# Masked keys of a small self-attention as four diagonal blocks, and a new slot order for its steps

## The chip, the cores and the metric

The kernel runs on one core of one Trainium2 chip. The engines of the core are TensorE (PE in the profile, with PEld for its weight loads), VectorE (DVE), ScalarE (ACT), GpSimd (POOL) and SyncE (SP, which issues the DMAs here). The metric is the device time of the program in microseconds, the median of several runs; lower is better.

## The reference

The program computes six residual steps on x (64 sequences of 32 tokens, width 256): cross-attention, windowed self-attention, a quantised FFN, a second cross-attention, a causal self-attention with a geometric bias, and a four-matrix FFN. The fifth is the one that the change touches:

```
qkv = (x @ Wqkv + bqkv)                       # x: layer-normed, 64 x 32 x 256; 16 heads of 16
std_logits   = einsum('bhid,bhjd->bhij', q, k) * dh ** (-0.5)
p1, p2       = x @ W1p, x @ W2p               # 4 numbers per head
lines_h      = plucker_lines(p1, p2)          # 6 products per head, divided by their norm
plucker_bias = einsum('bhic,bhjc->bhij', lines_h, lines_h @ _J6.T)
logits       = std_logits + plucker_bias * plucker_scale
attn = softmax(where(causal, -inf, logits));  out = (attn @ v) @ Wout + bout
```

## The kernel before, in words

Tokens lie in 16 tiles of 128 rows, four sequences of 32 tokens each. The fifth step, called A1 in the code, handles the tiles one after the other in four **lanes** (tile n is lane n mod 4); each lane has its own buffers and its own pair of PSUM banks, `bank[l][0]` and `bank[l][1]`. For each tile, in this order:

- ScalarE normalises x (`a_scale`), TensorE turns the tile (`p_turn`), ScalarE copies it (`a_xnT`), and TensorE multiplies by all weights (`p_project`; L548 and L554).
- VectorE puts q and k with their bias into slots of 32 columns per head (`d_slots`). ScalarE copies p1 and p2 out (`a_lines`), GpSimd forms the six products (`lines`, L2083 to L2089), VectorE sums their squares (`d_lines`), and GpSimd takes the norm's inverse and writes the line numbers into the slots (`lines_unit`, L2093 to L2102). GpSimd also adds the output bias (`bias`, L1948).
- TensorE turns the slots of q and k into the two banks (`p_slots`, L598 and L603). Now each 32-row group of `bank[l][1]` holds the keys of one head in a group of four heads. ScalarE copies the queries (`a_keys`, L1085). VectorE writes the **masked keys** (`d_keys`, L1407): a tile `kbd` of 128 x 2048 that repeats the keys four times and multiplies them by a 0/1 mask, so that only the diagonal 32-row blocks are not zero.
- TensorE multiplies (`p_scores`, L617). VectorE masks, takes the maximum and subtracts it (`d_mask` L1451, `d_max` L1456, `d_shift` L1460), ScalarE takes the exponential (`a_exp`, L1124), VectorE the sums (`d_sums`).
- TensorE turns the probabilities (`p_turn_probs`, L638), ScalarE copies them (`a_pT`, L1128), TensorE multiplies by the values (`p_values`, L648), VectorE normalises (`d_norm_out`, L1474), TensorE turns (`p_turn_out`, L657), ScalarE copies (`a_oT`), TensorE multiplies by Wout (`p_out`, L554), and VectorE adds to x (`d_add`, L1488). The values themselves are copied by ScalarE (`a_values`), turned by VectorE (`d_turn_values`) and spread by ScalarE (`a_spread_values`, L1074).

Each engine runs its own list in order and waits on semaphores. The order is set by a table of **slots**: a round has 28 slots, each lane starts 7 slots after the one before, and each engine has a list of (slot, step). So with T for the tile whose scores are next, each engine repeats one fixed sequence of steps of neighbouring tiles per 7 slots. Slots of two engines are not tied to each other except by the semaphores. `between` tables put single steps of the last FFN's start into the last round: the row statistics of the first block (`two_stats`, `g_aggregate`, `g_rsqrt`, `g_normalise`) and its first matmuls (`g_turn`, `g_pair`).

```
SLOTS0, SLOTS1 = 20, 28
lag = slots // NL
kbd = [view(a[2], 2048) for a in lane_at]
om = [view(a[2], D) for a in lane_at]
```

`om`, the normalised output of `d_norm_out`, lies over the first 256 columns of `kbd`.

Of the kernel before, what the change touches and what calls it, by code (L numbers as in the profile page):

```python
# [15 lines left out]
P = 128  # L16
# [27 lines left out]
def perceiver(nc, A, out):  # L44
    ctx = ExitStack()
    with ctx:
# [75 lines left out]
        om = [view(a[2], D) for a in lane_at]  # L122
        kT = [view(a[3], D) for a in lane_at]
# [278 lines left out]

        def halves(ap):
            return ap.rearrange("p (a b) -> p a b", b=P)
# [134 lines left out]
        def _(pe):  # L539
# [23 lines left out]
            def p_project(kind, l, n):  # L563
# [3 lines left out]
                if kind == A1:  # L567
                    project_rows(bank[l][0], xnT[l], a1_wqkv[:, :, 0:2 * D]).then_inc(s["qk_ready"], 1)
                    project_rows(bank[l][1][:, D:D + 8 * H], xnT[l],
                                 a1_wpl[:, :, :, :].rearrange("p k a b -> p k (a b)"))  # L570
                    for fo in range(KI):
                        r = project(vb[:, fo, :], a1_wqkv[:, :, 2 * D:3 * D], xnT[l], fo)
                    r.then_inc(s["v_ready"], 1)
                    return
# [78 lines left out]
            def p_turn_out(kind, l, n):  # L653

                pe.wait_ge(s["o_normed"], tile(n, l))
                for half in range(KI):
                    r = tr(bank[l][0][:, D + half * P:D + (half + 1) * P], om[l][:, half * P:(half + 1) * P], ident[:])  # L657
                r.then_inc(s["oT_ready"], 1)
# [351 lines left out]
            def g_last(b):  # L1010
                for t in range(TPB):
                    pe.wait_ge(g_c, quadrant_no(8 * b + 7, 12 if t >= 2 else 21))
                    at = slice(t % 2 * P, t % 2 * P + P)
                    for k in range(NF1):
# [7 lines left out]
                                (4, lambda l, i: p_project_last(A1, l, i + BASE[A1]))]  # L1022
                 + attention(A1, "a1", [(12, p_slots), (15, p_scores), (20, p_turn_probs),
                                        (22, p_values), (24, p_turn_out), (26, p_out)])[1])],
# [22 lines left out]
        def _(act):  # L1047
# [34 lines left out]
            def a_keys(kind, l, n):  # L1082
                if kind == A1:
                    act.wait_ge(s["qk_slots_ready"], tile(n - BASE[A1], l))
                    af(qT1[l], bank[l][0], ACT.Copy).then_inc(s["qT_copied"], 1)  # L1085
                    return
# [263 lines left out]
            def g_close(b, h, f):  # L1350
# [13 lines left out]
                (1, a_scale), (5, a_xnT), (9, a_lines), (12, a_values), (16, a_spread_values),  # L1364
                (18, a_keys), (23, a_exp), (24, a_pT), (27, a_oT))])], {("tail", 6): lambda: g_turned(0)})
# [17 lines left out]
        def _(dve):  # L1383
# [17 lines left out]
            def d_keys(kind, l, i, n):  # L1401

                if kind == A1:
                    dve.wait_ge(s["qk_slots_ready"], tile(n - BASE[A1], l))
                    k = bank[l][1].rearrange("p (c k) -> p c k", k=L).unsqueeze(2).broadcast_to([P, H, J, L])
                    m = mask4[:, :].unsqueeze(1).unsqueeze(3).broadcast_to([P, H, J, L])
                    v.tensor_tensor(kbd[l].rearrange("p (c j k) -> p c j k", j=J, k=L), k, m, ALU.mult)\  # L1407
                        .then_inc(s["k_masked"], 1)
# [61 lines left out]
            def d_norm_out(kind, l, i, n):  # L1470
# [3 lines left out]
                v.tensor_tensor(om[l].rearrange("p (h e) -> p h e", e=HD),  # L1474
# [323 lines left out]
            dve.wait_ge(consts_made, 6)  # L1798
# [4 lines left out]
            d_turn_values(A1, 0, 0, BASE[A1])  # L1803
            c_add(T - 1)
# [97 lines left out]
            def g_last(b):  # L1902
# [7 lines left out]
                (3, d_slots), (8, d_lines), (8, d_turn_values), (13, d_keys), (16, d_mask),  # L1910
                (16, d_max), (17, d_shift), (18, d_sums), (22, d_norm_out), (26, d_add))])],
# [16 lines left out]
        def _(pool):  # L1928
# [131 lines left out]
            for i in range(1, T - 1):  # L2060
                for u in range(SPT):
                    c_step(i, u, False, False)
                    n = SPT * i + u
                    for m, n0 in enumerate((8, 28)):
                        if n0 <= n < n0 + 8:
                            quadrant_sum(m, n - n0)
            for u, l in enumerate((0, 1, 3, 2)):
# [5 lines left out]
            pool.wait_ge(consts_made, 6)  # L2073
# [42 lines left out]
            def g_rsqrt(b):  # L2116
# [7 lines left out]
                (14, of_last(lines)), (17, lambda l, i: b_bias(A1, l, i)), (18, of_last(lines_unit))])],  # L2124
                      {("last", 18): lambda: g_rsqrt(0)})
# [90 lines left out]
```

## Time and profile before

| | us |
|---|---|
| median of 3 runs | 1551.03 (1550.93 to 1554.02) |
| the profiled execution, its own time | 1552.65 |
| its span, first to last instruction | 1550.8 |
| PE busy in the span | 1454.3 (94%) |
| DVE busy | 893.5 (58%) |
| ACT busy | 711.6 (46%) |
| POOL busy | 504.1 (33%) |

A1 stands between about 830 and 997 us of the span. Shares over the whole span say little about it: it is a sixth of the time and has its own limits, so it is read by its own chain of waits and timeline. "The granted clock" is the share of full speed that TensorE had in a stretch.

### The profile page before, as it was taken

What the parts mean: (1) busy time and instruction counts of PE and PEld (TensorE: products, weight loads), DVE (VectorE), ACT (ScalarE), POOL (GpSimd) and SP (SyncE); (2) the same over time, 40 slices, a digit from 0 to 9 for tenths busy, and PEclk for the clock granted to TensorE, in tenths of its full rate; (3) what the DMA queues carried; (4) which work ended last, traced back from release to release, by engine and by line L of the source; (5) the groups of instructions that cost most, each with busy time, mean ns of one, the idle gap of its engine ahead of it and who ended that gap; (6) DMA issues with size and microseconds to landing.
All of it is one profiled execution on the core that took longest, in us unless ns stands there. A gap on an engine that the chain in (4) does not pass through costs nothing.

```text
span 1550.8 us, 32878 instructions
## 1 busy us (share of the span) xinstructions
PE 1454.3 (94%) x12566; PEld 1126.0 (73%) x12566; DVE 893.5 (58%) x1892; ACT 711.6 (46%) x1767; POOL 504.1 (33%) x698
## 2 busy tenths in 40 slices
PE   6999998998999999999997888899999999999998
PEld 5877776456777777777775666578858876885887
DVE  5988997499446666666665887543234224323332
ACT  6887777498545555555553655322211211221221
POOL 2445552001037956965656777100000000000000
PEclk9999999999999999999998999999999999999999
DMA  8000000007031262146110000124404421441240
GB/s 304 21 7 2 1 1 21 0 7 220 18 145 54 69 249 60 42 169 230 48 41 1 2 0 2 49 87 139 155 14 142 143 109 48 143 143 62 95 143 14
DMA packets 60521, 124.13 MB, mean 80 GB/s; under 512 B 5009, under 2 KB 15761, under 8 KB 57873
## 3 DMA queue, kind: packets, MB, share of 16 engines
q1 hardware_dynamic: 60432, 122.94, 23.0%
q8 instruction: 57, 0.93, 0.3%
q14 instruction: 32, 0.25, 0.1%
HBM read 108.24 MB, written 14.68 MB: 79 GB/s over the span
## 4 chain that ended last, share of the span: by engine, by line
PE 69%; DVE 14%; POOL 8%; issue 5%; ACT 3%; DVEq 0%; DMA 0%; SPq 0%; POOLq 0%; ACTq 0%
PE ps L965 24%; PE ps L548 15%; PE ps L768 5%; PE ps L554 5%; PE ps L762 4%; PE ps L1016 4%; PE ps L788 3%; POOL R L2051 2%; PE ps L740 2%; POOL R L2033 2%; DVE R L1727 2%; DVE R L1407 2%; PE ps L799 2%; DVE amax L1594 1%; POOL R L2025 1%
## 5 line engine op out<-in xcount | busy, mean ns | idle before, releaser
L965 PE MATMUL ps<-R 128*128 128x256 f32 x1792 | 388.6, 379 | 3.4 <-DVE R L1875 3.4
L965 PEld LDWEIGHTS ps<-R 128*128 128x128 f32 x1792 | 340.0, 190 | 52.3 <-issue 6.5
L548 PE MATMUL ps<-R 128*128 128x128 f32 (+1 forms) x1344 | 306.3, 387 | 1.8 <-ACT R L1080 0.9
L548 PEld LDWEIGHTS ps<-R 128*128 128x128 f32 x1344 | 189.7, 194 | 110.2 <-issue 105.2
L1283 ACT ACTIVATE R<-ps,c_nmx 128x257 f32<-128x257 f32 x256 | 118.2, 474 | 126.4 <-DVE c_nmx L1751 126.4
L2033 POOL TENSOR_TENSOR R<-R,c_inv 128x1024 f32<-128x1024 f32 x64 | 121.1, 1892 | 130.9 <-DVE c_inv L1762 130.9
L1727 DVE COPY R<-ps 128x512 f32<-128x512 f32 x128 | 88.2, 689 | 82.3 <-PE ps L788 81.0
L768 PE MATMUL ps<-x_wv,R 128*128 128x256 f32 x512 | 121.1, 379 | 0.0
L2119 POOL TENSOR_SCALAR g_ve<-g_mv 128x4 f32<-128x4 f32 x4 | 1.0, 238 | 336.2 <-DVE g_mv L1824 336.2
L768 PEld LDWEIGHTS ps<-x_wv,R 128*128 128x128 f32 x512 | 92.5, 190 | 10.1
L762 PE MATMUL ps<-R,x_wk 128*128 128x256 f32 x384 | 95.6, 391 | 0.0
L1355 ACT ACTIVATE R<-R,ffn_s 128x256 f32<-128x256 f32 x32 | 16.3, 509 | 167.8 <-DVE R L1882 167.8
L788 PE MATMUL ps<-ident,R 128*128 128x128 f32 x512 | 80.1, 280 | 7.9 <-POOL R L2033 3.8
L1751 DVE TENSOR_REDUCE c_nmx<-ps 128x2 f32<-128x514 f32 x128 | 82.5, 686 | 1.6 <-PE ps L778 1.5
L762 PEld LDWEIGHTS ps<-R,x_wk 128*128 128x128 f32 x384 | 68.9, 189 | 12.2 <-issue 0.4
L788 PEld LDWEIGHTS ps<-ident,R 128*128 128x128 f32 x512 | 61.0, 142 | 21.7 <-issue 7.8
L1342 ACT ACTIVATE R<-ps,ffn_s 128x512 f32<-128x512 f32 x32 | 21.9, 687 | 114.9 <-PE ps L548 114.5
L1275 ACT ACTIVATE R<-ps 128x512 f32<-128x512 f32 x64 | 38.4, 600 | 75.3 <-PE ps L768 75.3
L1594 DVE TENSOR_REDUCE amax<-R 128x1 f32<-128x512 f32 (+1 forms) x60 | 58.3, 1002 | 23.7 <-ACT R L1170 23.2
L2025 POOL TENSOR_TENSOR R<-R 128x512 f32<-128x512 f32 x64 | 67.3, 1053 | 9.0 <-DMA R<-in_ctxT 9.0
L799 PEld LDWEIGHTS ps<-R 128*32 128x32 f32 x2048 | 32.4, 110 | 43.4 <-DVE R L1727 31.7
L1860 DVE SCALAR_TENSOR_TENSOR R<-ps,ffn_s,R 128x512 f32<-128x512 f32 x32 | 24.0, 750 | 59.4 <-ACT R L1342 59.4
(219 smaller groups left out, 2515.1 us busy)
## 6 DMA issues: line engine op xcount, KB each, us to landing
R<-quadrant_sums SPq DMA_DIRECT2D x32, 1024.0 KB, 6.8
R<-in_f_hq SPq DMA_DIRECT2D x32, 768.0 KB, 4.5
R<-in_ctxT SPq DMA_DIRECT2D x64, 257.0 KB, 2.7
R<-in_f_hq SPq DMA_DIRECT2D x8, 1024.0 KB, 8.7
quadrant_sums<-R SPq DMA_DIRECT2D x8, 1024.0 KB, 8.2
R<-in_ctxT SPq DMA_DIRECT2D x16, 256.0 KB, 3.9
k_ahead<-R SPq DMA_DIRECT2D x16, 256.0 KB, 3.8
R<-k_ahead SPq DMA_DIRECT2D x16, 256.0 KB, 3.1
```

What stands on the lines that cost most here:

```text
L548: r = mm(dst, w[:, ki, fo * P:(fo + 1) * P], src[:, ki, :], start=(ki == 0), stop=(ki == KI - 1))
L554: r = mm(dst, src[:, ki, :], w[:, ki], start=(ki == 0), stop=(ki == KI - 1))
L762: r = mm(ps[:, 4, fo * D:(fo + 1) * D], x1_wk[:, ki, fo * P:(fo + 1) * P], c_ctx[u][:, ki, 0:2 * P], start=(ki == 0), stop=(ki == KI - 1))
L768: r = mm(ps[:, 5, c * D:(c + 1) * D], c_ctx[u][:, ki, c * P:(c + 1) * P], x1_wv[:, ki, :], start=(ki == 0), stop=(ki == KI - 1))
L788: r = tr(ps[:, 6, at:at + P], c_p[par][:, g, c * P:(c + 1) * P], ident[:])
L965: r = mm(ps[:, 4 * (g % 2) + bk, half * HALF:(half + 1) * HALF], f_wr[g % 3][:, w, ki * P:(ki + 1) * P], src[:, k, ki, :], start=(ki == 0) ...
L1283: af(c_p[par][:, g, :], ps[:, g, 0:S], ACT.Exp, bias=c_nmx[par][:, g:g + 1], accum_out=c_sum[par][:, g:g + 1]).then_inc(c_exp, 1)
L1594: v.tensor_reduce(o, i, AX.X, ALU.max, apply_absolute_value=True).then_inc(f0_ugm, 1)
L1727: v.tensor_copy(c_pT[:, 2 * k:2 * k + 2, :, :].rearrange("p g c t -> p (g c t)"), ps[:, 6, :])\
L1751: v.tensor_reduce(c_nmx[u % 2][:, 2 * half:2 * half + 2], ps[:, 2 * half:2 * half + 2, 0:S], AX.X, ALU.max, negate=True).then_inc(c_max, 1)
L2025: p.tensor_tensor(c_ctx[u][:, :, 0:S - 1], c_ctx[u][:, :, 0:S - 1], c_ctx[u][:, :, S - 1:S].broadcast_to([P, KI, S - 1]), ALU.subtract).th ...
L2033: p.tensor_tensor(c_p[u % 2][:, :, 0:S - 1], c_p[u % 2][:, :, 0:S - 1], c_inv[u % 2][:, :].unsqueeze(2).broadcast_to([P, G, S - 1]), ALU.m ...
```

## The change

Instead of one multiplication by the mask, the masked keys become four copies of a diagonal block of 32 rows x 16 heads x 32 columns, from PSUM into `kbd`. VectorE copies blocks 0 and 1, ScalarE blocks 2 and 3 (behind its copy of the queries). The rest of `kbd` is zero: it is written once per lane by a memset of 128 x 2048, two on GpSimd inside the second cross-attention (after its sequences 48 and 52), one on GpSimd behind the last slot memset, one on VectorE in front of `c_add` of the last tile. So that nothing overwrites the zeros, A1's normalised output moves to `om1`, over the scores' buffer. `p_project` gets a wait for the x update of the lane's tile before. All four engines get other slots.

```
+        om1 = [view(a[5], D) for a in lane_at]
...
+        def key_block(l, j):
+            return kbd[l][j * L:(j + 1) * L, :].rearrange("p (c j k) -> p c j k", j=J, k=L)[:, :, j, :]
+        def key_rows(l, j):
+            return bank[l][1][j * L:(j + 1) * L, :].rearrange("p (c k) -> p c k", k=L)
...
                 if kind == A1:
+                    pe.wait_ge(s["x_updated"], tile(n - 1, l))
                     project_rows(bank[l][0], xnT[l], a1_wqkv[:, :, 0:2 * D]).then_inc(s["qk_ready"], 1)
...
-                                (4, lambda l, i: p_project_last(A1, l, i + BASE[A1]))]
-                 + attention(A1, "a1", [(12, p_slots), (15, p_scores), (20, p_turn_probs),
-                                        (22, p_values), (24, p_turn_out), (26, p_out)])[1])],
+                                (2, lambda l, i: p_project_last(A1, l, i + BASE[A1]))]
+                 + attention(A1, "a1", [(11, p_slots), (15, p_scores), (18, p_turn_probs),
+                                        (21, p_values), (23, p_turn_out), (26, p_out)])[1])],
...
                     act.wait_ge(s["qk_slots_ready"], tile(n - BASE[A1], l))
-                    af(qT1[l], bank[l][0], ACT.Copy).then_inc(s["qT_copied"], 1)
+                    af(qT1[l], bank[l][0], ACT.Copy)
+                    for j in (2, 3):
+                        r = af(key_block(l, j), key_rows(l, j), ACT.Copy)
+                    r.then_inc(s["qT_copied"], 1)
...
-                    v.tensor_tensor(kbd[l].rearrange("p (c j k) -> p c j k", j=J, k=L), k, m, ALU.mult)\
-                        .then_inc(s["k_masked"], 1)
+                    for j in (0, 1):
+                        r = v.tensor_copy(key_block(l, j), key_rows(l, j))
+                    r.then_inc(s["k_masked"], 1)
...
+            v.memset(kbd[3], 0.0).then_inc(consts_made, 1)
             c_add(T - 1)
...
-                (3, d_slots), (8, d_lines), (8, d_turn_values), (13, d_keys), (16, d_mask),
-                (16, d_max), (17, d_shift), (18, d_sums), (22, d_norm_out), (26, d_add))])],
+                (2, d_slots), (5, d_lines), (8, d_turn_values), (11, d_keys), (15, d_mask),
+                (15, d_max), (15, d_shift), (18, d_sums), (19, d_norm_out), (27, d_add))])],
...
+                    if n in (48, 52):
+                        p.memset(kbd[(n - 48) // 4], 0.0).then_inc(consts_made, 1)
...
-                (14, of_last(lines)), (17, lambda l, i: b_bias(A1, l, i)), (18, of_last(lines_unit))])],
-                      {("last", 18): lambda: g_rsqrt(0)})
+                (4, of_last(lines)), (12, lambda l, i: b_bias(A1, l, i)), (9, of_last(lines_unit))])],
+                      {("last", 16): lambda: g_rsqrt(0)})
```

ScalarE's table changes in the same way. What the tables do to the lists is seen in the program's rows. On TensorE, one repetition in the middle of A1 before: the probabilities' turn (L638) stands behind the output product (L554 with `a_wout`) and the slots (L598, L603).

```order
L617 MATMUL ps<-R 32x2x2x32 [waits qT_copied,k_masked]
L657 MATMUL ps<-ident,R 128x128 [waits o_normed]
L554 MATMUL ps<-a_wqkv,R 128x512 [waits xnT_copied]
L554 MATMUL ps<-a_wpl,R 128x128 x2
L548 MATMUL ps<-R,a_wqkv 128x128 x4
L554 MATMUL ps<-a_wout,R 128x256 [waits oT_copied]
L598 MATMUL ps<-ident,R 128x128 [waits q_slots]
L603 MATMUL ps<-ident,R 128x128 [waits v_copied]
L638 MATMUL ps<-ident,R 128x128 [waits probs_ready]
L560 MATMUL ps<-ident,R 128x128 [waits xn_ready]
L648 MATMUL ps<-R 32x4x16 [waits pT_copied,v_spread]
```

And the same repetition now (lines are 8 to 10 higher; L626 is the scores, L562 the products, L647 the probabilities' turn, L607 and L612 the slots, L657 the values, L568 the first turn):

```order
L626 MATMUL ps<-R 32x2x2x32 [waits qT_copied,k_masked]
L666 MATMUL ps<-ident,R 128x128 [waits o_normed]
L562 MATMUL ps<-a_wqkv,R 128x512 [waits x_updated,xnT_copied]
L562 MATMUL ps<-a_wpl,R 128x128 x2
L556 MATMUL ps<-R,a_wqkv 128x128 x4
L647 MATMUL ps<-ident,R 128x128 [waits probs_ready]
L607 MATMUL ps<-ident,R 128x128 [waits q_slots]
L612 MATMUL ps<-ident,R 128x128 [waits v_copied]
L562 MATMUL ps<-a_wout,R 128x256 [waits oT_copied]
L657 MATMUL ps<-R 32x4x16 [waits pT_copied,v_spread]
L568 MATMUL ps<-ident,R 128x128 [waits xn_ready]
```

The probabilities' turn moved ahead of the slots, and the output product behind them. On GpSimd in the last round, before, the FFN's row statistics (L2119, L2121) stand in front of a tile's `lines` (L2083):

```order
L2097 TENSOR_TENSOR R<-R,lrn 128x96 [waits q_evac,lines_step]
L2101 COPY R<-R 128x16x6 [waits lines_step]
L2102 TENSOR_TENSOR R<-R,plsc 128x16x6
L2119 TENSOR_SCALAR g_ve<-g_mv 128x4 [waits mv_ready]
L2121 TENSOR_TENSOR g_rstd<-g_ve,minus_half 128x4 [waits vare_ready]
L2083 TENSOR_TENSOR R<-R 128x16x3 [waits lines_in]
```

Now the same pair (L2139, L2141) stands one tile later, between `lines_unit` of tile 13 and `lines` of tile 14:

```order
L2117 TENSOR_TENSOR R<-R,lrn 128x96 [waits q_evac,lines_step]
L2121 COPY R<-R 128x16x6 [waits lines_step]
L2122 TENSOR_TENSOR R<-R,plsc 128x16x6
L2139 TENSOR_SCALAR g_ve<-g_mv 128x4 [waits mv_ready]
L2141 TENSOR_TENSOR g_rstd<-g_ve,minus_half 128x4 [waits vare_ready]
L2103 TENSOR_TENSOR R<-R 128x16x3 [waits lines_in]
```

Before, the pair was between tiles 12 and 13; the DVE statistics that it waits for stood behind `d_keys` of tile 12 and now stand in front of `d_mask` of tile 12.

## Rows read from the trace of the kernel before

**Rows 1.** Busy time by engine in one stretch: us, PE, PEld, DVE, ACT, POOL, PEclk, DMA

```profile
900.00:910.00 10.00, 8.52 (x132) 6.70 (x132) 8.70 (x18) 5.46 (x15) 7.41 (x15) 1.00 0.00 0
```

**Rows 2.** Chain of waits, one repetition of A1: start us, us, what

```profile
909.03 1.08 PE ps L617 x32
910.11 0.37 PE ps L657 x2
910.48 2.16 PE ps L554 x8
912.64 0.89 PE ps L548 x8
913.54 0.86 PE ps L554 x4
914.40 0.44 PE ps L598 x4
914.84 0.45 PE ps L603 x4
915.31 2.30 DVE R L1407
...
949.79 0.45 PE ps L638 x4
```

**Rows 3.** Timeline in the middle of A1: start us, us, engine, line, op, [idle before <-releaser]

```profile
897.48 1.42 POOL L2083 TENSOR_TENSOR R<-R 128x48 f32<-128x48 f32 x6 [0.96 <-ACT R L1111]
...
901.05 2.91 POOL L2093 TENSOR_TENSOR lrn<-lsq,minus_half 128x16 f32<-128x16 f32 x1 [0.57 <-DVE lsq L1436]
...
901.55 0.69 DVE L1451 SCALAR_TENSOR_TENSOR R<-ps,causal 128x512 f32<-128x512 f32 x1 [0.21 <-PE ps L617]
...
903.72 0.63 ACT L1124 ACTIVATE R<-R 128x512 f32<-128x512 f32 x1 [0.93 <-DVE R L1460]
...
904.78 0.37 POOL L2102 TENSOR_TENSOR R<-R,plsc 128x96 f32<-128x96 f32 x1
...
907.12 0.60 ACT L1128 ACTIVATE R<-ps 128x512 f32<-128x512 f32 x1 [1.01 <-PE ps L638]
907.62 0.60 ACT L1085 ACTIVATE R<-ps 128x512 f32<-128x512 f32 x1
...
907.86 0.65 PE L648 MATMUL ps<-R 128*32 128x64 f32 x32 [0.56 <-ACT R L1128]
```

**Rows 4.** Groups of instructions by line: busy us, mean ns of one | idle before

```profile
L1727 DVE COPY R<-ps 128x512 f32<-128x512 f32 x128 | 88.2, 689 | 82.3 <-PE ps L788 81.0
L2072 POOL MEMSET R<- 128x1024 f32 x4 | 3.8, 952 | 0.0
L1074 ACT ACTIVATE R<-R,mask 128x256 f32<-128x256 f32 x64 | 27.1, 494 | 2.3 <-DVE R L1419 2.3
```

**Rows 5.** Timeline: around two of the places where memsets go

```profile
744.20 1.89 POOL L2033 TENSOR_TENSOR R<-R,c_inv 128x1024 f32<-128x1024 f32 x1 [0.26 <-DVE c_inv L1762]
...
748.48 0.60 PE L788 MATMUL ps<-ident,R 128*128 128x128 f32 x4
...
843.03 0.42 DVE L1745 TENSOR_TENSOR x<-x,ps 128x256 f32<-128x256 f32 x1 [2.51 <-PE ps L554]
```

**Rows 6.** Timeline: scores of tiles 1, 12 and 13 on PE

```profile
857.10 1.08 PE L617 MATMUL ps<-R 128*32 128x128 f32 x32 [0.51 <-DVE R L1407]
...
952.18 1.08 PE L617 MATMUL ps<-R 128*32 128x128 f32 x32 [0.52 <-DVE R L1407]
...
965.24 1.08 PE L617 MATMUL ps<-R 128*32 128x128 f32 x32
```

**Rows 7.** Timeline: the row statistics on GpSimd, and TensorE after them

```profile
952.61 0.25 POOL L2119 TENSOR_SCALAR g_ve<-g_mv 128x4 f32<-128x4 f32 x1 [4.23 <-DVE g_mv L1824]
952.94 1.04 POOL L2121 TENSOR_TENSOR g_rstd<-g_ve,minus_half 128x4 f32<-128x4 f32 x1
...
960.89 1.11 PE L598 MATMUL ps<-ident,R 128*128 128x128 f32 x4 [3.34 <-POOL R L2101]
```

More of the change, by code:

```diff
@@ L656, in p_turn_out @@
                 for half in range(KI):
-                    r = tr(bank[l][0][:, D + half * P:D + (half + 1) * P], om[l][:, half * P:(half + 1) * P], ident[:])
+                    r = tr(bank[l][0][:, D + half * P:D + (half + 1) * P], (om1 if kind == A1 else om)[l][:, half * P:(half + 1) * P],
+                           ident[:])
                 r.then_inc(s["oT_ready"], 1)
@@ L1084, in a_keys @@
                     act.wait_ge(s["qk_slots_ready"], tile(n - BASE[A1], l))
-                    af(qT1[l], bank[l][0], ACT.Copy).then_inc(s["qT_copied"], 1)
+                    if isinstance(n, int) and n == BASE[A1]:
+                        act.wait_ge(consts_made, 10)
+                    af(qT1[l], bank[l][0], ACT.Copy)
+                    for j in (2, 3):
+                        r = af(key_block(l, j), key_rows(l, j), ACT.Copy)
+                    r.then_inc(s["qT_copied"], 1)
                     return
@@ L1363, in _ @@
             run_lanes(act, SLOTS1, [(lambda: None, [(at, of_last(step)) for at, step in (
[L1364 to L1365 removed]
+                (0, a_scale), (3, a_xnT), (9, a_lines), (11, a_values), (18, a_spread_values),
+                (17, a_keys), (20, a_exp), (24, a_pT), (27, a_oT))])], {("tail", 6): lambda: g_turned(0)})
             for l in range(NL):
@@ L1404, in d_keys @@
                     dve.wait_ge(s["qk_slots_ready"], tile(n - BASE[A1], l))
-                    k = bank[l][1].rearrange("p (c k) -> p c k", k=L).unsqueeze(2).broadcast_to([P, H, J, L])
-                    m = mask4[:, :].unsqueeze(1).unsqueeze(3).broadcast_to([P, H, J, L])
-                    v.tensor_tensor(kbd[l].rearrange("p (c j k) -> p c j k", j=J, k=L), k, m, ALU.mult)\
-                        .then_inc(s["k_masked"], 1)
+                    if isinstance(n, int) and n == BASE[A1]:
+                        dve.wait_ge(consts_made, 10)
+                    for j in (0, 1):
+                        r = v.tensor_copy(key_block(l, j), key_rows(l, j))
+                    r.then_inc(s["k_masked"], 1)
                     return
@@ L1473, in d_norm_out @@
                 dve.wait_ge(s["o_ready"], tile(n, l))
-                v.tensor_tensor(om[l].rearrange("p (h e) -> p h e", e=HD),
+                v.tensor_tensor((om1 if kind == A1 else om)[l].rearrange("p (h e) -> p h e", e=HD),
                                 bank[l][0][:, 0:D].rearrange("p (h e) -> p h e", e=HD),
@@ L1797, in _ @@
             c_evacuate(NSEQ - 1, 0)
-            dve.wait_ge(consts_made, 6)
+            dve.wait_ge(consts_made, 8)
             d_slots(A1, 0, 0, BASE[A1])
@@ L2072, in _ @@
                 p.memset(slots_of[l], 0.0).then_inc(consts_made, 1)
-            pool.wait_ge(consts_made, 6)
+            p.memset(kbd[2], 0.0).then_inc(consts_made, 1)
+            pool.wait_ge(consts_made, 8)
             pool.wait_ge(later_made, 3)
```

## The prediction, made before the changed kernel was run

> **What bounds the kernel now.** I read the self-attention stage A1 alone, in four steps. First the busy time by engine in one stretch of ten microseconds [rows 1]: TensorE 8.52, VectorE 8.70, GpSimd 7.41, ScalarE 5.46. No engine is full, so the stage is bound by a loop of waits that passes over engines, and the chain of waits has to show it. It does [rows 2]: from the start of one tile's scores (L617) to the next tile's it reads scores 1.08, turn of the output 0.37, projections 2.16 + 0.89, output product 0.86, the two turns of the slots 0.44 + 0.45, the masked keys on VectorE 2.30, and then scores again. That is 8.55 us and 0.08 between the pieces, 8.63 a tile. The scores of tiles 1 and 12 start at 857.10 and 952.18 [rows 6]: 95.08 over 11 tiles, 8.64. So the loop holds for the whole middle, and of its parts only the keys are not TensorE's. While they are made, TensorE does what it has (turns, values) and idles for the rest; part of it is a wait of 0.56 for the copied probabilities [rows 3].
>
> Second, the end of the stage. Between the scores of tiles 12 and 13 lie 13.06 us [rows 6], 4.42 more than a period. GpSimd stood 4.23 us in front of the row statistics of the next FFN, which wait for VectorE behind the keys of tile 12; so it began the lines of tile 13 late, and TensorE stood 3.34 us for the slots of tile 13. After that its four turns took 1.11 us, where the chain gives 0.44 in the middle [rows 2, 7]: a wait of this length is also paid in clock.
>
> **The keys.** The one instruction of 2.30 us on the loop goes. VectorE gets two copies of 32 x 512 from PSUM, ScalarE two of the same size behind its copy of the queries. No row shows 32 partitions at work. The nearest for VectorE is its copy of 128 x 512 from PSUM, 0.689 [rows 4]; two are 1.38. For ScalarE two copies of 128 x 512 from PSUM stand back to back, each of 0.60 and 0.50 apart [rows 3]; three in a row take 0.50 + 0.50 + 0.60 = 1.60. Both start when the slots are turned, so ScalarE ends last and 1.60 takes the place of 2.30. From below: were fewer partitions cheaper, the queries' copy alone still takes 0.60, and TensorE's own work between the slots and the scores would decide (below). From above: the spread of the values writes short runs, 0.494 for 256 elements [rows 4], so 0.99 for 512; then ScalarE takes 0.50 + 2 x 0.99 = 2.5. I take 1.60, since engine, source and size are those of its rows and only the partitions differ.
>
> The trace has 2.30 for 2048 elements in one instruction and 0.689 for 512, so four pieces cost 2.76 of engine time. The Trainium skill warns of this on the page "VectorE: DVE Perf Modes" (section "The TRN2 errata — SBUF-src ops pay a fixed extra latency per instruction"): the fixed cost is paid by each instruction, so many small tiles are dear. Were all four pieces on VectorE, the keys' step would be 2.76 and the loop longer than now; by the rows it shrinks only because two engines work side by side.
>
> **The loop after the new slots.** TensorE's list now has the turn of the probabilities (0.45) where the output product (0.86) was; the product stands behind the slots, beside the keys. The loop is 1.08 + 0.37 + 2.16 + 0.89 + 0.45 + 0.44 + 0.45 = 5.84, plus 1.60 for the keys and 0.08: **7.52 us**. Beside the keys TensorE has the product 0.86, the values 0.65 at most and one turn of about 0.2, in sum 1.7: as long as the keys. So its own work is about as long as the loop, and nothing much below 7.4 can come of it. What else has to be ready in time:
> - Probabilities. From the mask (901.55) to the exponential's end (903.72 + 0.63) it is 2.80 [rows 3]; with 0.07 ahead and 0.05 behind, 2.92 after the scores. The cover was turn, projections, product and slots; now it is the turn and the projections, 0.37 + 3.05 = 3.42. Hidden, with 0.5 to spare; behind this wait stand the slots, the product, the values and the next scores.
> - VectorE: 8.70 in ten is 7.5 a tile; less 2.30, plus 1.38 makes 6.6 of 7.52. ScalarE: 4.7 plus 1.2 makes 5.9. ScalarE's exponential now stands behind spread, values and the output's copy of its list; these end about 2.8 us after the scores' start, the shift ends at 3.3.
> - GpSimd: lines and bias from 897.48 to 900.48 (901.05 less the idle 0.57), 3.00, and the unit from 901.05 to 905.15, 4.10 [rows 3]: 7.1 of 7.52. It fits, but with only 0.4 a tile.
> - The new wait for the x update in front of the projections: that addition ends some five microseconds before, it costs nothing. Behind it stands all of TensorE's list.
> Gain: 8.64 - 7.52 = 1.12 a tile.
>
> **The memsets.** A memset of 1024 on GpSimd takes 0.952 [rows 4]; 2048 lie between that and 1.90. The first, behind sequence 48, would push the normalisation at 744.20 by at most 1.64; it would end at 747.7, and TensorE turns its result at 748.48 [rows 5]: hidden, with 0.75 left. The same pattern repeats behind sequence 52. The third stands where GpSimd waits for A1's first lines. If that cover were gone, each would cost up to 1.9. VectorE's memset is not in the trace; a 2048-element instruction takes 2.30 there [rows 2], and it falls into an idle stretch of 2.51 in front of L1745 [rows 5]. I count all four as nothing.
>
> **The sum.** From the scores of tile 1 to those of 14 are 13 periods: 13 x 1.12 = 14.6. The excess of 4.4 at tile 13 goes, since GpSimd meets the statistics one tile later, when VectorE has long made them. Put back: two pairs of statistics and the aggregation on VectorE, which has less room now, about 0.6; and GpSimd's 0.25 + 1.04 with gaps = 1.4 [rows 7], against 0.4 of room a tile, about 0.8 at tile 14. The last two tiles, whose steps alternate with matmuls of the FFN, gain 0.7 each on their keys, and TensorE waits about 0.4 more for the last probabilities, whose turn now stands ahead of a product: +1.0. The first tile's keys: +0.7. In sum 14.6 + 4.4 - 1.4 + 1.0 + 0.7 = **19.3 us**. The profiled execution's span goes from 1550.8 to 1531.5 and its time from 1552.65 to 1533.4. The median was 1.6 below the latter, 1551.03, so the forecast is **1531.7**. A measurement of this kernel can tell about 0.2%, 3.1 us, from no change.
>
> **Rivals.**
> 1. The small room is used up, and another engine's loop ends last. GpSimd has 0.4 a tile, the probabilities 0.5. VectorE's sums of squares wait for GpSimd's lines, and the next tile's mask stands behind them; if they come 0.9 us late, TensorE waits at the probabilities each time. For it: GpSimd was idle 0.96 + 0.57 a tile, and 1.1 of that goes with the period. Against: the sum of its work is below 7.52. With a period of 7.9 and 1.9 put back at the end: 13 x 0.74 + 4.4 - 1.9 + 1.0 + 0.7 = 13.8, so 1537.2.
> 2. ScalarE's blocks cost 1 us each, by their written pattern (0.494 for 256), or because both engines now read one PSUM bank at a time, which they don't do before, and ScalarE waits 1.38 for VectorE: keys of 2.5, period 8.4. 13 x 0.24 + 4.4 - 0.5 + 0.7 = 7.7, so 1543.3. 
> 3. Better: the end puts nothing back and the period is TensorE's own 7.4: 13 x 1.24 + 4.4 + 1.0 + 0.7 = 22.2, so 1528.8.
> 4. Slower than before: a block of 32 rows costs ScalarE 1.5 us, three times what its size says. Then the keys take 3.5, the period is 5.84 + 3.5 + 0.08 = 9.4, and 13 x 0.78 = 10.1 is lost against 4.4 won: 1556.7. A tile gets longer from a block of 1.1 us (5.84 + 0.50 + 2.2 + 0.08 = 8.6), and the whole from 1.3, where 13 x 0.4 outweighs the stall's end. Against: the dearest row of ScalarE per element [rows 4] gives 0.99.
>
> **How the numbers follow.** Forecast 0.50, first rival 0.23, second 0.10, third 0.09, fourth 0.03; 0.05 for an end within 0.2%, where a period near 8.4 meets memsets that are not hidden. The forecast with the first and third rival makes 0.82, and reaches, with 1.5 us for their own spread, from 1527.5 to 1540; the second's bound is partly in it up to a period of 8.1, so I take 1527 to 1541. Faster by over 0.2%: 0.91, within: 0.05, slower: 0.04.
>
> **What would show it.** In the profile after: ScalarE's block copies at 0.60 and VectorE's at 0.69; the scores of tiles 2 to 12 at 7.5 apart; in the chain the keys' step on ScalarE's line, or no keys at all where TensorE's work fills it; no wait of GpSimd at the statistics and none of 3 us at the slots of tile 13; the second cross-attention as long as before. A period with a wait of the probabilities' turn (L647) or of the slots (L607) in it means the first rival, block copies of 1 us the second. The forecast is wrong if the gain isn't in A1's middle.

## The result

| | before, us | after, us |
|---|---|---|
| median | 1552.25 (4 runs) | 1537.4 (4 runs, 1535.16 to 1539.34) |
| profiled execution, own time | 1552.65 | 1535.16 |
| its span | 1550.8 | 1533.4 |

The ratio is 0.9906, with a 95% interval of 0.9893 to 0.992: 14.6 us less (0.94%). Between the two profiled executions it is 17.5. The prediction was 1531.7 with a range of 1527 to 1541 and a gain of 19.3. Direction and range held; the median is 5.7 above the forecast time, and the gain is 4.7 less than forecast.

The busy time of the same stretch as in [rows 1], in the changed kernel (columns as there: PE, PEld, DVE, ACT, POOL, clock):

```profile
900.00:910.00 10.00, 9.68 (x164) 7.23 (x166) 8.40 (x20) 8.68 (x21) 8.34 (x18) 1.00 0.00 0
```

TensorE went from 8.52 to 9.68 of ten: it is nearly the bound now. ScalarE went from 5.46 to 8.68. The chain of waits, one repetition, answers [rows 2] (L626 scores, L666 turn of the output, L562 and L556 projections, L647 turn of the probabilities, L607 and L612 slots, L1097 queries and L1099 two key blocks on ScalarE):

```profile
917.08 1.08 PE ps L626 x32
918.16 0.37 PE ps L666 x2
918.53 2.16 PE ps L562 x8
920.70 0.89 PE ps L556 x8
921.59 0.44 PE ps L647 x4
922.03 0.44 PE ps L607 x4
922.46 0.45 PE ps L612 x4
922.94 0.60 ACT R L1097
923.55 0.59 ACT R L1099
924.15 0.60 ACT R L1099
924.75 0.14 issue
924.88 1.08 PE ps L626 x32
```

This is the loop of the prediction, piece by piece, with two differences: the keys take 1.80 and not 1.60, and 0.14 follows them. 7.80 us in sum. The timeline of the same place shows what else stood near the end of the loop: VectorE's two blocks took their 1.38 and were done at 924.32, TensorE's own list was done at 924.72, ScalarE at 924.74.

```profile
922.94 0.60 ACT L1097 ACTIVATE R<-ps 128x512 f32<-128x512 f32 x1 [0.28 <-PE ps L612]
922.94 1.38 DVE L1423 COPY R<-ps 32x512 f32<-32x512 f32 x2 [0.70 <-PE ps L612]
923.55 1.19 ACT L1099 ACTIVATE R<-ps 32x512 f32<-32x512 f32 x2
923.70 0.65 PE L657 MATMUL ps<-R 128*32 128x64 f32 x32
924.28 0.44 PE L568 MATMUL ps<-ident,R 128*128 128x128 f32 x2
924.88 1.08 PE L626 MATMUL ps<-R 128*32 128x128 f32 x32 [0.16 <-ACT R L1099]
```

I took the start of the scores of every tile from the timelines and give the steps between them, for all kernels that follow too (one execution of each). "End" is from the scores of tile 15 to the start of the last output product, "sum" from the scores of tile 1 to there (before: 857.10 to 995.71; after: 854.89 to 978.28).

| kernel | mean of 1 to 11 | 11-12 | 12-13 | 13-14 | 14-15 | end | sum |
|---|---|---|---|---|---|---|---|
| before | 8.64 | 8.63 | 13.06 | 8.62 | 11.23 | 10.62 | 138.61 |
| after | 7.78 | 8.10 | 8.10 | 8.62 | 9.29 | 11.49 | 123.39 |
| after, second set of runs | 7.78 | 8.09 | 8.10 | 8.62 | 9.30 | 11.49 | 123.40 |
| blocks in the old order | 9.28 | 9.15 | 11.38 | 9.15 | 9.18 | 10.64 | 142.35 |
| the same, turn first | 8.64 | 8.66 | 11.92 | 8.74 | 9.19 | 10.64 | 135.57 |
| new order, one product | 8.25 | 8.76 | 8.75 | 8.64 | 10.92 | 11.49 | 131.07 |
| before, g_rsqrt later | 8.64 | 8.63 | 8.63 | 8.63 | 9.51 | 10.63 | 132.48 |
| two blocks left out | 7.59 | 7.57 | 7.56 | 8.15 | 9.90 | 11.49 | 120.59 |
| ScalarE's blocks from the queries' bank | 7.78 | 8.09 | 8.09 | 8.65 | 10.97 | 11.48 | 125.10 |
| ScalarE's blocks 128 rows | 7.59 | 8.10 | 8.10 | 8.62 | 9.52 | 11.49 | 121.76 |
| ScalarE's blocks, same rows | 7.66 | 8.10 | 8.10 | 8.63 | 9.42 | 11.48 | 122.32 |
| four blocks on VectorE | 9.00 | 11.20 | 9.51 | 8.72 | 9.67 | 11.49 | 140.60 |
| statistics before the keys | 7.78 | 7.79 | 7.80 | 8.28 | 9.29 | 11.49 | 122.44 |
| statistics earlier still | 7.78 | 7.80 | 8.60 | 7.80 | 9.29 | 11.49 | 122.79 |

So A1 from the scores of tile 1 on is 15.2 us shorter in this pair of profiles. The step from tile 0 to tile 1 went from 9.47 to 9.11. The other 1.8 us between the two profiled spans lie ahead of A1's scores, in a stretch whose steps on TensorE are the same in both kernels. Busy time and clock of that stretch, before and after:

```profile
800.00:830.00 30.00, 24.94 (x338) 18.37 (x337) 18.45 (x44) 14.62 (x50) 16.26 (x16) 0.90 0.04 10
```

```profile
800.00:830.00 30.00, 24.16 (x340) 18.13 (x339) 18.52 (x45) 14.60 (x50) 16.73 (x16) 0.97 0.04 10
```

The granted clock was 0.90 in the one and 0.97 in the other. In the second set of runs of the changed kernel the first scores started at 847.45, where the profile above has 845.78 and before 847.63, and A1 was the same to 0.01 us. That part is no gain of the change.

The step 14-15 holds a second difference of this kind. In the kernel before and in the same kernel with only `g_rsqrt` later, TensorE waits as long for the slots of this step (2.05 and 2.04), and then the same four matmuls take:

```profile
981.22 3.47 PE L548 MATMUL ps<-R 128*128 128x512 f32 x4
```

```profile
977.81 1.88 PE L548 MATMUL ps<-R 128*128 128x512 f32 x4
```

The granted clock was 0.68 in the first (979.70 to 985.09) and 1.00 in the second (976.40 to 980.09). The changed kernel and the one whose ScalarE reads the queries' bank differ in the same way without any stall before: 9.29 at a clock of 1.00 (961.50 to 966.79), 10.97 at 0.75 (963.70 to 970.66), behind equal waits of 1.61. So of the 1.94 that the step 14-15 fell from before to after, about 1.6 is clock (3.47 less 1.88), and no run shows it to belong to the change. Both clock differences widen the gap between the two profiled executions (17.5) beyond that of all runs (14.6).

### The profile page after: what moved, and what is told of

It reads as the page before. It is cut to its first block, busy times and chain, and to the rows that moved or that the text cites. A ratio compares the mean times of both kernels' runs of the same rounds, so it can differ in the third digit from the quotient of the medians.

```text
span 1533.4 us, 32957 instructions
## 1 busy us (share of the span) xinstructions
PE 1450.5 (95%) x12566; PEld 1122.4 (73%) x12566; DVE 880.5 (57%) x1909; ACT 732.6 (48%) x1799; POOL 507.2 (33%) x701
## 4 chain that ended last, share of the span: by engine, by line
PE 69%; DVE 12%; POOL 9%; issue 5%; ACT 3%; DVEq 0%; DMA 0%; SPq 0%; POOLq 0%; ACTq 0%
PE ps L975 24%; PE ps L556 15%; PE ps L778 5%; PE ps L562 4%; PE ps L772 4%; PE ps L1026 4%; PE ps L798 3%; POOL R L2068 2%; PE ps L750 2%; DVE R L1743 2%; POOL R L2050 2%; PE ps L809 2%; DVE amax L1610 1%; POOL R L2042 1%; PE ps L657 1%
## 5 line engine op out<-in xcount | busy, mean ns | idle before, releaser
L556 PE MATMUL ps<-R 128*128 128x128 f32 (+1 forms) x1344 | 305.2, 386 | 1.8 <-ACT R L1090 0.9
L556 PEld LDWEIGHTS ps<-R 128*128 128x128 f32 x1344 | 189.7, 194 | 109.8 <-issue 104.6
L2139 POOL TENSOR_SCALAR g_ve<-g_mv 128x4 f32<-128x4 f32 x4 | 0.9, 236 | 331.1 <-DVE g_mv L1841 331.1
```

The lines of the kernel that those rows point to most:

```text
L556: r = mm(dst, w[:, ki, fo * P:(fo + 1) * P], src[:, ki, :], start=(ki == 0), stop=(ki == KI - 1))
```

## The end of the stage

In the last tiles the chain leaves the loop of TensorE and ScalarE and goes over GpSimd (L2103 to L2109 the lines, L1965 the bias, L2113 to L2122 the unit):

```profile
929.78 1.42 POOL R L2103 x6
...
932.08 0.68 POOL x L1965
932.76 1.00 issue
933.80 2.92 POOL lrn L2113
936.79 0.36 POOL R L2117
...
937.90 1.41 POOL R L2103 x6
```

From one tile's lines to the next tile's it is 8.12 us. The "issue" of 1.00 is a wait for VectorE's sums of squares, which stand behind the FFN's row statistics. The timeline names it, beside the statistics that cause it:

```profile
932.15 0.75 DVE L1835 BATCH_NORM_STATS2 g_stats<-x 128x6 f32<-128x256 f32 x2
932.93 0.42 DVE L1490 TENSOR_TENSOR R<-ps,rinv 128x256 f32<-128x256 f32 x1
933.80 2.91 POOL L2113 TENSOR_TENSOR lrn<-lsq,minus_half 128x16 f32<-128x16 f32 x1 [1.04 <-DVE lsq L1452]
```

In the middle this wait is 0.39. GpSimd's own two instructions, which stood behind a wait of 4.23 in [rows 7], now stand behind none; but the x update behind the lines comes late, and TensorE waits for it:

```profile
946.09 0.25 POOL L2139 TENSOR_SCALAR g_ve<-g_mv 128x4 f32<-128x4 f32 x1
946.42 1.04 POOL L2141 TENSOR_TENSOR g_rstd<-g_ve,minus_half 128x4 f32<-128x4 f32 x1
...
949.76 0.25 DVE L1450 TENSOR_REDUCE lsq<-R 128x16 f32<-128x96 f32 x1 [0.85 <-POOL R L2109]
...
950.36 0.41 DVE L1504 TENSOR_TENSOR x<-x,ps 128x256 f32<-128x256 f32 x1
...
950.92 1.95 PE L562 MATMUL ps<-a_wqkv,R 128*128 128x512 f32 x4 [0.59 <-DVE x L1504]
```

## Experiments: which part of the change gives the gain

**Blocks alone.** The changed kernel with all slots of the kernel before.

```
-(11, p_slots), (15, p_scores), (18, p_turn_probs), (21, p_values), (23, p_turn_out), (26, p_out)
+(12, p_slots), (15, p_scores), (20, p_turn_probs), (22, p_values), (24, p_turn_out), (26, p_out)
...
-(18, a_spread_values), (17, a_keys), (20, a_exp), (24, a_pT), (27, a_oT)
+(16, a_spread_values), (18, a_keys), (23, a_exp), (24, a_pT), (27, a_oT)
```

> The changed kernel with the four blocks, om1 and the memsets, but with all slots of the kernel before (g_rsqrt at slot 18 too). Theory 1, each part is worth what its own place in the loop says: the keys' step shrinks from 2.30 to the 1.80 that ScalarE's three copies take in the trace of after (0.60 each, end to end), the rest of the loop stays, so the period is 8.13 and not 8.64; 13 x 0.5 = 6.5 us and about 1 more at the first and last tiles; the stall in front of the scores of tile 13 (13.06 for one tile before) stays near 12.6, and GpSimd stands over 4 us at the row statistics. About 1545, 7 us below before. Theory 2, the blocks pay only together with the order (another wait of the old list, such as the probabilities, fills the 0.5): period near 8.6, time within 1.5 us of before.

Measured: 1559.73 against 1552.15, ratio 1.0056 (1.0035 to 1.0076). The blocks alone make the kernel slower by 7.6 us, and both theories missed: a tile takes 9.15 and not 8.13. The timeline shows why (L647 turn of the probabilities, L1143 their copy):

```profile
903.16 0.60 PE L612 MATMUL ps<-ident,R 128*128 128x128 f32 x4
...
903.59 0.60 PE L647 MATMUL ps<-ident,R 128*128 128x128 f32 x4
903.80 1.38 DVE L1423 COPY R<-ps 32x512 f32<-32x512 f32 x2 [0.22 <-PE ps L612]
...
904.23 0.60 ACT L1143 ACTIVATE R<-ps 128x512 f32<-128x512 f32 x1 [1.02 <-PE ps L647]
904.73 0.59 ACT L1097 ACTIVATE R<-ps 128x512 f32<-128x512 f32 x1
```

VectorE starts its blocks at 903.80. ScalarE's list has the copy of the probabilities ahead of the keys, and this copy waits for TensorE's turn, which stands behind the slots. So ScalarE idles 1.02 and begins the queries at 904.73, 0.93 behind VectorE; from there its 1.80 decide. Before, ScalarE's queries were a single short copy beside 2.30 on VectorE, and this queue cost nothing. The blocks put ScalarE on the loop, and with it whatever is queued ahead of them.

**One place of TensorE's list.** The old order again, with the turn of the probabilities ahead of the slots.

```
-(12, p_slots), (15, p_scores), (20, p_turn_probs)
+(12, p_slots), (15, p_scores), (19, p_turn_probs)
```

> The four blocks in the order of before, with one place of TensorE's list changed: the turn of the probabilities stands ahead of the slots' turns (slot 19 and not 20), behind the output product. Theory 1: in the old order ScalarE's keys were queued behind its copy of the probabilities, which waited for TensorE's turn behind the slots; with the turn ahead of the slots that copy is done when the slots are, the queries' copy starts 0.06 to 0.3 behind them, and the period falls from 9.15 to 5.84 + 0.86 + 1.80 + 0.14 = 8.64; about 1553 to 1554, as much as before. Theory 2, ScalarE's list is not what costs: the probabilities are not ready ahead of the slots (2.92 after the scores), TensorE waits there, and the period stays at 9.1.

Measured: 1550.09 against 1551.03, ratio 0.9994 (0.998 to 1.0009), period 8.64 to the hundredth. Theory 1 holds for the period and for "as much as before"; its 1553 to 1554 was 3 to 4 too high (the steps 12-13 and 14-15 are 11.92 and 9.19, where before has 13.06 and 11.23). ScalarE's queue was the cost, and this one place of the new order pays for it. The rest of the way from 8.64 to 7.78 is as long as the output product (0.86), which the new order moves beside the keys; no run moves this product alone.

**Order alone.** The changed kernel with the masked keys as one product on VectorE.

```
-for j in (0, 1):
-    r = v.tensor_copy(key_block(l, j), key_rows(l, j))
...
+v.tensor_tensor(kbd[l].rearrange("p (c j k) -> p c j k", j=J, k=L), k, m, ALU.mult)
...
-for j in (2, 3):
-    r = af(key_block(l, j), key_rows(l, j), ACT.Copy)
```

> The changed kernel with its new slots and om1, but the masked keys as one multiplication of 128 x 2048 on VectorE, as before; ScalarE copies only the queries. Theory 1: the loop is after's with 2.30 in the place of 1.80, so 7.79 + 0.50 = 8.29 a tile; 0.35 a tile is won on before over 11 tiles (3.8), and the stall of 4.4 at tile 13 is gone because GpSimd meets the statistics a tile later; less 1 to 2 us in the last tiles. About 1545.5, 6 to 7 us below before, and with the gain of the blocks in the old order the sum is near the 14.6 of the whole change. Theory 2: the order brings only the stall (the turn of the probabilities, 0.45, takes the place of the output product, but VectorE is too full): period 8.6, about 1548.

Measured: 1546.49 against 1552.15, ratio 0.9964 (0.9955 to 0.9974), 5.7 us less; periods of 8.25. Theory 1 holds. The two parts don't add up, they need each other: in the old order the blocks change the period from 8.64 to 9.15, in the new one from 8.25 to 7.78.

**The stall at tile 13.** The kernel before with one number changed.

```
-{("last", 18): lambda: g_rsqrt(0)}
+{("last", 25): lambda: g_rsqrt(0)}
```

> The kernel before with one number changed: GpSimd's g_rsqrt stands at slot 25 of the last round and not at 18, so one tile later. Theory 1: the excess of 4.4 us in front of the scores of tile 13 is this wait alone; it goes, GpSimd's two instructions cost about 1.3 us against 1.5 of room a tile (8.64 less 7.1), so 0 to 0.5 comes back a tile later: about 1548, 4 to 4.4 below before. Theory 2: the excess belongs to something else in the last round (the VectorE statistics, the clock): it stays or moves to tile 14, and the time is within 1 us of before.

Measured: 1547.6 against 1552.15, ratio 0.9978 (0.9968 to 0.9988), 4.6 us less. Theory 1 holds: 13.06 became 8.63, and nothing came back at tile 14. The step 14-15 also fell, from 11.23 to 9.51, but that is the granted clock shown under the table. So this number alone is worth 4.4 us in the trace, beside 4.6 in the medians, and that is about three tenths of the 15.2 by which A1 got shorter.

## Experiments: why a tile takes 7.78 and not 7.52

The queries' copy and the two blocks stand 0.60 apart. In [rows 3] two full copies stand 0.50 apart. What takes the overlap away?

**Another bank.** ScalarE's blocks read the queries' bank.

```
-r = af(key_block(l, j), key_rows(l, j), ACT.Copy)
+r = af(key_block(l, j), bank[l][0][j * L:(j + 1) * L, :].rearrange("p (c k) -> p c k", k=L), ACT.Copy)
```

> The changed kernel, but ScalarE's two block copies read rows 64 to 127 of the queries' bank and not of the keys' bank, so that VectorE and ScalarE no longer read one bank together; the values of two blocks are not the keys (that part of the result is changed), sizes and places written stay. Theory 1, the missing overlap (0.60 apart and not 0.50, so 1.80 for the three copies and not 1.60) comes with copies of 32 rows and not with the shared bank: still 1.80. Theory 2, the shared bank holds ScalarE up: 1.60, and 0.50 between the starts of copies.

```profile
901.71 0.60 ACT L1097 ACTIVATE R<-ps 128x512 f32<-128x512 f32 x1 [0.28 <-PE ps L612]
902.32 1.19 ACT L1099 ACTIVATE R<-ps 32x512 f32<-32x512 f32 x2
```

Still 1.80 and 7.78 a tile (one run, 1539.05; its longer step 14-15 is the clock of 0.75 told above). The shared bank costs nothing. The Trainium skill ("PSUM — Partial Sum Buffer", section "PSUM bank collisions raise a hardware error") has accesses to different groups of 32 rows of one bank as clean; this trace agrees, and the half of the second rival that rested on the bank falls.

**Full width.** Copies of 128 rows from the queries' bank.

```
-r = af(key_block(l, j), key_rows(l, j), ACT.Copy)
+r = af(kbd[l].rearrange("p (c j k) -> p c j k", j=J, k=L)[:, :, j, :],
+       bank[l][0].rearrange("p (c k) -> p c k", k=L), ACT.Copy)
```

> As the run on the other bank, with 128 rows in each of ScalarE's two block copies and the same 512 elements a row, written in the same runs of 32 (the off-diagonal blocks of two head groups are no longer zero, so the scores are changed). Theory 1, the overlap is lost with 32 rows: the copies start 0.50 apart, three take 1.60, and the scores start as TensorE's own work allows, a period of 7.71. Theory 2, the overlap is lost by the destination in runs of 32 columns: 0.60 apart again, 1.80, period 7.80.

```profile
900.14 0.60 ACT L1097 ACTIVATE R<-ps 128x512 f32<-128x512 f32 x1 [0.28 <-PE ps L612]
900.63 1.08 ACT L1099 ACTIVATE R<-ps 128x512 f32<-128x512 f32 x2
```

The copies stand 0.49 apart, three take 1.57, and TensorE shows no idle time ahead of the scores: 7.59 a tile (one run, 1535.0). The scores start 0.15 behind ScalarE's end, as in the changed kernel, so ScalarE's loop and TensorE's own list end together here. So four times the rows are quicker in sum. The written pattern is the same as in the block copies, so the pattern is not the cause either.

**32 rows, but the same ones twice.** Both copies at rows 64 to 95.

```
-r = af(key_block(l, j), key_rows(l, j), ACT.Copy)
+r = af(kbd[l][2 * L:3 * L, :].rearrange("p (c j k) -> p c j k", j=J, k=L)[:, :, j, :],
+       key_rows(l, 2), ACT.Copy)
```

> The changed kernel, but both of ScalarE's block copies read rows 64 to 95 of the keys' bank and write rows 64 to 95 (block 3 stays zero, and a second copy of block 2 stands beside it, so the scores are changed). Theory 1, the overlap is lost with 32 rows as such: 0.60 between the starts of the two copies, as in after. Theory 2, it is lost where the first row changes from one instruction to the next (0, then 64, then 96 in after): queries' copy to first block 0.60, but first to second block 0.50, so 1.70 for the three.

```profile
907.55 0.60 ACT L1097 ACTIVATE R<-ps 128x512 f32<-128x512 f32 x1 [0.28 <-PE ps L612]
908.16 1.07 ACT L1099 ACTIVATE R<-ps 32x512 f32<-32x512 f32 x2
```

From the queries (rows from 0) to the first block (from 64) it is 0.61, but the two copies of the same rows take 1.07 together, at 0.58 each: they overlap again. Three take 1.68. Theory 2 holds in its numbers: ScalarE's copies overlap by about 0.1 where the first row stays the same and not where it changes. The two block copies of the changed kernel (rows 64, then 96) have the size and the bank of these; only the rows differ. The Trainium skill ("ScalarE: Activation LUTs", section "What ACT_TABLE_LOAD costs") says that ScalarE's instructions overlap by about 93 ns back to back; this trace agrees where the first row stays, and not where it changes.

**TensorE alone.** Blocks 1 and 3 left out.

```
-for j in (2, 3):
+for j in (2,):
...
-for j in (0, 1):
+for j in (0,):
```

> The changed kernel without block 1 (VectorE) and block 3 (ScalarE): the keys' step shrinks to 1.20 on ScalarE and 0.69 on VectorE; half of the keys is left out of the scores. Theory 1, TensorE's own work behind the slots (product, values, turn, with what stands between them) is 1.9 us and now ends last: the period is 7.71, the same as between the few tiles of after where the scores had no wait, only 0.08 below after; about 1536.5. Theory 2, the keys' step decides and TensorE's own work is the 1.7 of the prediction, or less: the period falls to about 7.4 and the time to 1532.

Measured: 1532.3 against 1551.03, ratio 0.988 (0.9852 to 0.9909). The period is 7.59, so neither theory had the number. TensorE ends last here, as theory 1 says; but its list takes 7.59, and the 7.71 between some tiles of the changed kernel were no floor. ScalarE is done 0.5 ahead of the scores, and nothing more is won from quicker keys. The time fell by more than the middle gives (1.9 us); 1.1 of that are the steps 11-12 and 12-13, now 7.57 and 7.56. With one block less VectorE probably has the statistics' 0.75 to spare. Of the 0.26 by which a tile is longer than forecast, 0.19 is the lost overlap: with it back the period is 7.59. The other 0.07 is TensorE's own list; without that list ScalarE's loop would not be shorter, since its 1.57 is followed by 0.15 (5.83 + 0.03 + 1.57 + 0.15 = 7.58), where the kernel before has 0.05 between VectorE's keys and the scores.

**All four on VectorE.**

```
-for j in (2, 3):
-    r = af(key_block(l, j), key_rows(l, j), ACT.Copy)
...
-for j in (0, 1):
+for j in (0, 1, 2, 3):
```

> The changed kernel with all four blocks on VectorE and only the queries on ScalarE. Theory 1, VectorE's copies cost 0.69 each whatever stands beside them, so 2.76 where one product takes 2.30: the keys' step grows from 1.80 to 2.76, and the period from 7.79 to 8.7 or 8.8, longer than before's 8.64, while the stall at tile 13 stays away; VectorE's work is 6.6 + 1.4 = 8.0 a tile, so its own list may add some; about 1551 to 1553. Theory 2, copies one behind another on VectorE overlap as full-width ones on ScalarE do: under 2.4 in sum, period 8.3, about 1546.

Measured: 1555.87 against 1551.55, ratio 1.0028 (1.0015 to 1.0041); most periods are near 8.86. Theory 1 holds for the copies and errs about the end, where a step of 11.20 stands between tiles 11 and 12:

```profile
946.78 0.75 DVE L1833 BATCH_NORM_STATS2 g_stats<-x 128x6 f32<-128x256 f32 x2
...
948.27 0.42 DVE L1502 TENSOR_TENSOR x<-x,ps 128x256 f32<-128x256 f32 x1
948.83 1.85 PE L562 MATMUL ps<-a_wqkv,R 128*128 128x512 f32 x2 [0.35 <-DVE x L1502]
...
955.17 2.79 DVE L1421 COPY R<-ps 32x512 f32<-32x512 f32 x4 [1.11 <-PE ps L612]
```

The four copies take 2.79, where one product of the same 2048 elements took 2.30. The step of 11.20 begins with the new wait of the projections for the x update: VectorE's addition stands behind keys and statistics, TensorE waits 0.35, and then it runs at about half speed (two matmuls of the projection take 1.85, where four take 1.88 in the middle of after; the granted clock was 0.54 from 948.80 to 952.20). All four take 3.56 here, so 1.7 of the step is clock. The next step has the same wait of 0.35 behind the other pair of statistics and runs at full clock: 9.51.

## Experiments: the end of the stage

**Statistics before the keys.**

```
-("last", 4): lambda: two_stats(0), ("last", 11): lambda: two_stats(2),
+("last", 3): lambda: two_stats(0), ("last", 10): lambda: two_stats(2),
```

> The changed kernel, with the two pairs of row statistics of the FFN on VectorE (0.75 us each) one place earlier: in front of the sums and the keys of a tile, where VectorE is idle for 0.70, and not behind the keys, where they push the sums of squares that GpSimd waits for. Theory 1: scores 11 to 12 and 12 to 13 take 7.8 and not 8.10, GpSimd waits 0.4 and not 1.04 in front of L2113, and TensorE's wait of 0.59 for the x update at tile 14 shrinks; 0.6 to 1.2 us in all, about 1536.5. Theory 2: GpSimd's loop ends last at the end of the stage whatever VectorE does, as its room is used up by its own 7.1 us a tile: nothing changes, 1537.4.

Measured: 1536.43, ratio 0.9904 (0.9887 to 0.992). In the trace theory 1 holds: 8.10 and 8.10 became 7.79 and 7.80, 8.62 became 8.28, and A1 is 0.95 shorter. The time can't tell it from the changed kernel (1537.4 in its first runs, 1536.63 in the second set, ratio 0.9903).

**Statistics and g_rsqrt earlier still**, with the changed kernel once more beside it.

```
-("last", 4): lambda: two_stats(0), ("last", 11): lambda: two_stats(2), ("last", 14): lambda: g_aggregate(0)
+("last", 3): lambda: (two_stats(0), two_stats(2)), ("last", 7): lambda: g_aggregate(0)
...
-{("last", 16): lambda: g_rsqrt(0)}
+{("last", 9): lambda: g_rsqrt(0)}
```

> The changed kernel with the FFN's row statistics earlier still: both pairs in front of the sums and keys of one tile (1.5 us into VectorE's 0.70 of idle time), the aggregation behind the next addition, and GpSimd's g_rsqrt one tile earlier. Theory 1: VectorE's keys end 0.4 to 0.8 late once, against 0.4 that they have to spare beside ScalarE's 1.80; GpSimd's 1.3 us then have one more tile to be regained (0.3 + 0.4 of room in each), so the tile with 8.62 in front of scores 14 becomes 8.0 or less, and the two with 8.10 become 7.8: 1 to 1.5 us below the changed kernel. Theory 2: GpSimd's room is none at a period of 7.8, so the 1.3 stays wherever it stands, and the time is within 0.5 us of stats_before_keys.

> The changed kernel as it is, on the same chip as stats_earlier and four_on_dve, to compare them with. Every theory expects the 1537.4 of its first runs within 2 us, and scores 7.8 apart in the middle.

Measured: 1537.83, ratio 0.9915 (0.9901 to 0.9929), beside 1536.63 and 0.9903 (0.9887 to 0.9918) for the changed kernel. Theory 1 fails in its main point: the long step only moved, from 13-14 to 12-13, at 8.60. Theory 2 fits the trace, where A1 is 0.35 from the run before (122.79 and 122.44). The room of GpSimd doesn't add up over tiles. Its delay is handed on within the same tile:

```profile
941.09 0.25 DVE L1450 TENSOR_REDUCE lsq<-R 128x16 f32<-128x96 f32 x1 [0.83 <-POOL R L2109]
941.69 0.41 DVE L1504 TENSOR_TENSOR x<-x,ps 128x256 f32<-128x256 f32 x1
942.25 1.10 PE L562 MATMUL ps<-a_wqkv,R 128*128 128x512 f32 x2 [0.56 <-DVE x L1504]
```

VectorE's addition stands behind its sums of squares, which wait for GpSimd's late lines, and TensorE's projections wait for the addition. Between 0.5 us (statistics before the keys, 8.28) and 0.8 are lost wherever the 1.3 are put. No variant that keeps all the keys beats the changed kernel by more than its measurement can tell.

## Where the prediction was right, and where not

- **The loop.** Right in its parts: scores, turns, projections and slots stand in the chain with the times that the sum had, and VectorE's blocks took 0.681 each for 0.689. The period was 7.78 for 7.52. The term that was mis-sized is "three in a row take 0.50 + 0.50 + 0.60 = 1.60": a block copy did cost 0.60, but the overlap of full copies was taken over to copies that begin at other rows. Over 13 periods (13 x 0.86 = 11.2 for 14.6) this and the 0.07 of the floor are 3.4 us, most of the 4.7 by which the gain is short. The 0.08 between the pieces was also taken over from VectorE's keys; behind ScalarE's it is 0.17 (0.03 and 0.14).
- **TensorE's own work** beside the keys was put at 1.7, and the floor at 7.4. By the prediction's own terms it is 5.84 + 1.7 = 7.54. Two runs show 7.59, one of them with ScalarE done 0.5 ahead. The third rival (7.4) could not happen.
- **Why the order.** The prediction took the gain from TensorE's list and gave ScalarE's keys a start right behind the slots without asking what is queued ahead of them on ScalarE. In the new order that was true. That the blocks cost 7.6 us in the old one stood nowhere in it.
- **The stall.** Right in place and cause: GpSimd meets the statistics without a wait, and moving this step alone takes 13.06 to 8.63. Its size was right too, 4.43 for 4.4. The remark on the clock there compares two views: the four turns took 1.11 in the timeline, where the timeline gives 0.60 in the middle (0.44 is the chain's). And a wait does not settle the clock: behind two equal waits (2.05 and 2.04, in the step 14-15) it was 0.68 once and 1.00 once.
- **Work per engine.** ScalarE was put at 4.7 a tile from one stretch of ten microseconds. From 857.10 to 952.18 it was busy 57.00 us for 11 tiles, 5.2 each, and in the changed kernel 52.31 for 8 tiles (854.89 to 917.08), 6.5 for a forecast of 5.9. It is still below the period, so nothing followed from it.
- **What the end gives back.** 0.6 was put on VectorE's statistics and 0.8 on tile 14. Measured: the steps 11-12 and 12-13 are together 0.6 above 7.79, where VectorE's statistics make GpSimd's loop the last at 8.10, and the step 13-14 is 0.8 above. Both terms are right.
- **The last two tiles.** Forecast +1.0, measured 21.85 to 20.78, +1.1. That is luck. The 21.85 has the 1.6 us of lower clock in it; against the kernel with `g_rsqrt` later, which ran these tiles at full clock (20.14), the new order loses 0.6 here.
- **The first tile.** Forecast +0.7, measured 0.36 in the step from tile 0 to tile 1. What lies ahead of the first scores can't be told from the clock there.
- **The new wait** for the x update was put at nothing ("that addition ends some five microseconds before, it costs nothing"). It ends 0.4 before: in the middle the addition ends at 925.77 (L1504, 925.35 for 0.42) and the projections start at 926.17. In the middle the result is still nothing; in the step 13-14 it cost 0.59, and in two of the experiments it is how a delay of VectorE or GpSimd reaches TensorE.
- **The memsets.** Right. The first one pushed the normalisation behind it from 744.20 to 745.61, and TensorE's turn came at 748.45 (748.48 before):

```profile
L2085 POOL MEMSET R<- 128x2048 f32 x2 | 3.6, 1806 | 0.0
L2092 POOL MEMSET R<- 128x2048 f32 x1 | 1.8, 1805 | 0.0
L1820 DVE MEMSET R<- 128x2048 f32 x1 | 1.8, 1765 | 0.4 <-issue 0.4
```

- **The first rival** (13.8 us, 1537.2) gave nearly the measured time by another way. Its mechanism, a period of 7.9 set by GpSimd or the probabilities, is not what bounds the middle, where GpSimd had 0.7 of idle time a tile and the turn of the probabilities waited for nothing. GpSimd's loop was the last only for two tiles at the end. That a rival hits the number is no proof of its cause; the chain decided.

Left open: why the overlap on ScalarE depends on the first row, and whether the rows read or the rows written matter, since in every run both changed together; why 0.15 and not 0.05 lies between the last copy and the scores when TensorE has waited shortly or not at all (it is 0.05 behind ScalarE too in the old order, where TensorE waits 0.95); and what lowers the clock in the step 14-15 of some executions.

## What to carry to other kernels

Work that is moved to a second engine starts when that engine's queue lets it, so read what stands ahead of it there; a split can be a loss in one order and a gain in another. When pieces of an instruction are priced by a row, check that the row's neighbours begin at the same rows too, since overlap belongs to the pair and not to the instruction. And price a wait on another engine's next step by its distance in the timeline, also for the tiles in which something else delays that step.

## What the runs showed of the hardware that was not expected

- ScalarE's copies of 512 elements from PSUM stand 0.49 to 0.50 apart at 128 rows, 0.60 to 0.61 where the first row changes, and near 0.49 again at 32 rows if the first row stays. 32 rows cost as much as 128 (0.589 and 0.599 each).
- VectorE's 32-row copies, each at another first row, don't overlap: 0.68 to 0.69 each, four in 2.79. Whether the same rows would overlap was not tried.
- Zeroing 128 x 2048 takes 1.81 on GpSimd and 1.77 on VectorE, less than a product of the same size (2.30).
- The same steps behind the same wait of TensorE came once at a granted clock of 1.00 and once at 0.75 (9.29 and 10.97 us for the step 14-15). A step of one profile should be compared with another only beside the clock of both.
